# Experts' outputs weighed on the way out of PSUM and added into the tokens' rows in DRAM, with one row per token loaded in the last stage

## The reference

```python
w_topk = w_topk / (jnp.sum(w_topk, axis=-1, keepdims=True) + 1e-06)
...
valid = ranks < capacity
slot = flat_sel * capacity + ranks
...
h = jax.nn.gelu(jnp.einsum('ecd,edf->ecf', padded_x, w1), approximate=False)
out_padded = jnp.einsum('ecf,efd->ecd', h, w2).reshape(N_EXPERTS * capacity, D)
gather_idx = jnp.where(valid, slot, 0)
out_rep = jnp.where(valid[:, None], out_padded[gather_idx], 0.0)
out_w = out_rep * w_topk.reshape(-1)[:, None]
return out_w.reshape(T, TOP_K, D).sum(axis=1).reshape(B, S, D)
...
src = _rmsnorm(src, norm1_w)
src = src + _moe(src, gate_w, w1, w2)
return _rmsnorm(src, norm2_w)
```

## Time and profile before

| | |
|---|---|
| median of 3 runs | 3386.67 us (3379.31 to 3386.76) |
| the profiled execution | 3384.39 us |
| its span, first to last instruction | 3382.7 us |
| experts block | 2759.8 to 3305.1 us |
| combine block | 3305.1 to 3382.7 us |
| PE busy, share of the span | 93% |
| DVE, ACT, POOL busy | 62%, 49%, 33% |
| DMA mean | 110 GB/s; 242 MB read from HBM, 130 MB written |

### The profile page before, as it was taken

One profiled execution on the slowest core, in us unless ns is written; L12 is line 12 of the kernel. 1 busy time (PEld: TensorE's weight loads), 2 busy tenths in 40 slices (PEclk: granted clock), 3 DMA queues, 4 the chain that ended last, 5 costly groups with the idle time before them and its releaser, 6 DMA issues. The chain is left out here.

```text
span 3382.7 us, 58016 instructions
## 1 busy us (share of the span) xinstructions
PE 3135.4 (93%) x18353; PEld 1927.6 (57%) x18353; DVE 2082.6 (62%) x5622; ACT 1663.4 (49%) x3743; POOL 1118.9 (33%) x1508
## 2 busy tenths in 40 slices
PE   7899999999989976999999999999998859999997
PEld 3667767677665653344444444444443348888882
DVE  7777777777772233677777777777777632222226
ACT  3565565655641113666666666666665611111116
POOL 2132232322342123334444444444443322222224
PEclk9999999999999988999999999999999979999998
DMA  8110110101125841112222222222222137777758
GB/s 288 5 73 36 57 51 36 72 36 66 42 88 200 303 169 29 54 54 72 74 73 73 74 73 73 68 73 72 71 73 72 51 99 238 230 235 238 225 169 298
DMA packets 266210, 370.48 MB, mean 110 GB/s; under 512 B 41615, under 2 KB 201579, under 8 KB 263904
## 3 DMA queue, kind: packets, MB, share of 16 engines
q1 hardware_dynamic: 250592, 329.82, 30.2%
q0 software_dynamic: 14832, 34.57, 2.8%
q10 hardware_dynamic: 544, 3.15, 0.2%
HBM read 242.38 MB, written 130.39 MB: 110 GB/s over the span
## 5 line engine op out<-in xcount | busy, mean ns | idle before, releaser
L2425 ACT ACTIVATE pT<-psum 128x512 f32<-128x512 f32 x1024 | 599.1, 599 | 363.2 <-PE psum L3176 348.0
L2709 DVE TENSOR_REDUCE negmax<-psum 128x2 f32<-128x1024 f32 x512 | 624.7, 1220 | 213.8 <-PE psum L3146 198.8
L3176 PE MATMUL psum<-q_stack,k_stack 99*128 99x512 bf16 x1024 | 378.8, 383 | 19.0 <-ACT pT L2425 12.0
L3146 PE MATMUL psum<-k_stack,q_stack 96*128 96x512 bf16 x1024 | 308.1, 382 | 53.7 <-DVE negmax L2709 36.4
L944 ACT ACTIVATE probs<-probs,negmax 128x256 f32<-128x256 f32 x512 | 252.8, 495 | 138.6 <-DVE negmax L1036 135.0
L3492 ACT ACTIVATE actT_x<-psum 128x512 f32<-128x512 f32 x142 | 84.8, 597 | 445.0 <-PE psum L3558 445.0
L3522 DVE COPY ye<-psum 128x512 f32<-128x512 f32 x71 | 49.1, 691 | 400.0 <-PE psum L3570 400.0
L3188 PE MATMUL psum<-pT,v_tile 128*32 128x512 f32 x2048 | 274.3, 608 | 1.0 <-ACT pT L2425 1.0
L3480 POOL DMA_INDIRECT chosen_out<-ye,place x142 | 140.0, 986 | 401.1 <-DVE ye L3522 241.1
L3558 PE MATMUL psum<-xT_x,w_x 128*128 128x256 f32 x1136 | 259.3, 382 | 0.0
L3570 PE MATMUL psum<-w_x,actT_x 128*128 128x256 f32 x1136 | 256.6, 379 | 0.0
(11 more groups left out here) (391 smaller groups left out, 5865.4 us busy)
## 6 DMA issues: line engine op xcount, KB each, us to landing
w_x<-in_L_ffn_w_dram SPq DMA_DIRECT2D x142, 512.0 KB
w_e<-in_L_ffn_w_dram SPq DMA_DIRECT2D x46, 1024.0 KB, 7.2
q_stacks<-q_part SPq DMA_DIRECT2D x192, 128.0 KB
q_stack<-q_stacks SPq DMA_DIRECT2D x64, 384.0 KB, 3.5
padded<-w_e SPq DMA_DIRECT2D x32, 645.0 KB, 5.6
xe<-padded SPq DMA_DIRECT2D x71, 258.0 KB
gate_rows<-mods SPq DMA_DIRECT2D x66, 256.0 KB, 3.3
chosen_out<-w_e SPq DMA_DIRECT2D x16, 1024.0 KB, 7.5
```

What stands on the lines that cost most here:

```text
L2425: act.activation(pT[:, 4 * (s % 2) + r, :], bank(m, 2 + n % 2), ACT.Exp, scale=float(DHQ) ** -0.5)\
L2709: dve.tensor_reduce(negmax[:, p // 2, h:h + 2], m.psum[:, at:at + 2, :], AX.X, ALU.max, negate=True)\
L3146: mm = pe.matmul(bank(m, at + j), q_stack[0:K_SCORE, h, t * P:(t + 1) * P], k_stack[0:K_SCORE, g, :], start=True, stop=True)
L3176: pe.matmul(bank(m, 2 + n % 2), k_stack[:, g, kc * P:(kc + 1) * P], q_stack[:, REP * g + r, :], start=True, stop=True).then_inc(sT_done, 1)
```

## The change

A row of `padded_dram` becomes two numbers longer (260 instead of 258) and carries the token's two weights, and its token number counts tokens and not pairs. In the experts block `place_rows` becomes five small DVE operations, which also work out each row's weight (`weight`), and `copy_out` multiplies by it in two operations of 256 columns. The scatter goes to `src_dram` and adds there (`compute_op=ALU.add`). As two experts may have the same token, the first scatter of tile i waits until both of tile i-1 have landed; the second waits for the first half of the up product of tile i+2, no longer for both. SP waits for `weight` before it loads the rows of tile i+3. The loads of `src_all` leave the experts block.

In the combine block SP issues 16 loads of 512 KB of `src_dram`, all at the start. PE copies each batch to PSUM (no products with expert rows), ACT squares three of the four parts from SBUF, and DVE squares the fourth (`last_square`) and then does the root's steps and the scaling as before. `chosen_out`, its zero stores, the buffer `zeros` and its memset on POOL, and `gather_wt` are gone; in `place` a copy of the weights into `src` takes the place of `valid`, and the product for `gather_wt` is left out.

```diff
@@ routing and rows
-ROW = D + 2
+ROW = D + 4
...
-                sp.dma_start(chosen_out[bass.ds(b * (T * TOPK // B), T * TOPK // B), :]
-                             .rearrange("(p r) d -> p (r d)", p=P), zeros).then_inc(zero_filled, 16)
...
-            pool.memset(zeros, 0.0).then_inc(zeros_ready, 1)
...
-                step(dve.tensor_scalar(valid[:, :, :], rank_k[:, :, :], float(CAP), None, ALU.is_lt))
...
+                step(dve.tensor_copy(src[:, par, :, D + 2:D + 4], wk[:, :, :]))
...
-                step(dve.tensor_tensor(m.gather_wt[:, at], wk[:, :, :].rearrange("p t k -> p (t k)"),
-                                       valid[:, :, :].rearrange("p t k -> p (t k)"), ALU.mult))
@@ experts_block, sync
-                    sp.wait_ge(place_ready, i + 1)
+                    sp.wait_ge(weight_ready, 3 * i + 3)
...
-                if i % 4 == 2 and i // 4 < B:
-                    b = i // 4
-                    sp.dma_start(m.src_all[:, b, :, :], src_dram[b * S:(b + 1) * S, :]
-                                 .rearrange("(t p) d -> p t d", p=P)).then_inc(src_in, 16)
@@ experts_block, gpsimd
                 for t in range(RT):
+                    if t == 0 and i:
+                        pool.wait_ge(sent[(i - 1) % WB], 16 * RT * ((i - 1) // WB + 1))
...
                     if t == 1 and i + 2 < NTILEX:
-                        pool.wait_ge(up_done, 2 * (i + 2) + 2)
-                    pool.indirect_dma_start(chosen_out,
+                        pool.wait_ge(up_done, 2 * (i + 2) + 1)
+                    pool.indirect_dma_start(src_dram,
                                             bass.IndirectOffsetOnAxis(ap=place[:, i % WB, t:t + 1], axis=0),
-                                            ye[:, i % WB, t, :], None, bounds_check=T * TOPK - 1, oob_is_err=False)\
+                                            ye[:, i % WB, t, :], None, bounds_check=T - 1, oob_is_err=False,
+                                            compute_op=ALU.add)\
@@ experts_block, vector
-                dve.tensor_tensor(place[:, u, :], second[:, u, :], xe[:, u, :, D], ALU.add).then_inc(place_ready, 1)
+                dve.tensor_copy(place[:, u, :], xe[:, u, :, D]).then_inc(place_ready, 1)
...
+                dve.tensor_tensor(change[:, :], xe[:, u, :, D + 3], xe[:, u, :, D + 2], ALU.subtract)\
+                    .then_inc(weight_ready, 1)
+                dve.wait_ge(weight_ready, 3 * i + 2)
+                dve.tensor_tensor(change[:, :], change[:, :], second[:, :], ALU.mult).then_inc(change_ready, 1)
+                dve.wait_ge(change_ready, i + 1)
+                dve.tensor_tensor(weight[:, u, :], change[:, :], xe[:, u, :, D + 2], ALU.add).then_inc(weight_ready, 1)
...
-                dve.tensor_copy(ye[:, i % WB, :, :].rearrange("p t d -> p (t d)"), bank(m, 4 + i % 2))\
-                    .then_inc(ye_ready, 1)
+                dve.wait_ge(weight_ready, 3 * i + 3)
+                for t in range(RT):
+                    ins = dve.tensor_scalar(ye[:, i % WB, t, :], bank(m, 4 + i % 2)[:, t * D:(t + 1) * D],
+                                            weight[:, i % WB, t:t + 1], None, ALU.mult)
+                ins.then_inc(ye_ready, 1)
@@ combine_block
-                sp.dma_start(got[:, b % GB, :, :, :].rearrange("p t k d -> p t (k d)"),
-                             chosen_out[b * S * TOPK:(b + 1) * S * TOPK, :]
-                             .rearrange("(t p k) d -> p t (k d)", p=P, k=TOPK)).then_inc(got_in[b % GB], 16)
+                sp.dma_start(m.src_all[:, b, :, :], src_dram[b * S:(b + 1) * S, :].rearrange("(t p) d -> p t d", p=P))\
+                    .then_inc(src_in[b], 16)
...
-                    act.activation(got[:, b % GB, t, 0, :], got[:, b % GB, t, 0, :], ACT.Copy,
-                                   scale=m.gather_wt[:, j:j + 1]).then_inc(first_ready, 1)
...
-                    dve.scalar_tensor_tensor(out=y(b, t), in0=got[:, b % GB, t, 1, :], scalar=m.gather_wt[:, j:j + 1],
-                                             in1=y(b, t), op0=ALU.mult, op1=ALU.add).then_inc(y_ready, 1)
...
+                dve.tensor_tensor_reduce(last[:, :], y(b, NT - 1), m.src_all[:, b, NT - 1, :], scale=1.0 / D, scalar=0.0,
+                                         op0=ALU.mult, op1=ALU.add, accum_out=mean_sq[:, b % 2, NT - 1:NT])\
+                    .then_inc(ms_dve, 1)
```

More of the change, by code:

```diff
@@ L3405, in experts_block @@
         own_f = sb("own_f", [P, RT])
-        second = sb("second", [P, WB, RT])
+        second = sb("second", [P, RT])
+        change = sb("change", [P, RT])
+        weight = sb("weight", [P, WB, RT])
         place = sb("place", [P, WB, RT], U32)
@@ L3638, in store @@
                     .then_inc(stored, 16)
-            for b in range(GB):
+            for b in range(B):
                 load(b)
             for b in range(B):
-                if b + GB < B:
-                    sp.wait_ge(y_ready, (b + 1) * NT)
-                    load(b + GB)
-                if b >= 2:
-                    store(b - 2)
-            store(B - 2)
-            store(B - 1)
+                store(b)
             sp.wait_ge(stored, 16 * B)
@@ L3694, in seed @@
                     act.wait_ge(z_ready, (b - 1) * NT)
[L3695 to L3699 removed]
+                act.wait_ge(src_in[b], 16)
+                for t in range(NT - 1):
+                    act.activation(square[:, t, :], m.src_all[:, b, t, :], ACT.Square, scale=1.0 / 16.0,
+                                   accum_out=mean_sq[:, u, t:t + 1]).then_inc(ms_act, 1)
+                act.wait_ge(ms_act, (b + 1) * (NT - 1))
+                act.wait_ge(ms_dve, b + 1)
                 act.activation(log_ms[:, u, :], mean_sq[:, u, :], ACT.Ln, bias=eps[:, 0:1]).then_inc(log_ready, 1)
```

88 lines of the change are left out of this document (35 added, 53 removed).

## The result

The changed kernel takes 3366.48 us, median of 7 runs (3364.71 to 3373.18), against 3386.76 for the kernel before (3379.31 to 3389.57): a ratio of 0.9946, 95% interval 0.9937 to 0.9955. A second measurement on another chip gave 0.9938 (0.9924 to 0.9951). The profiled execution took 3366.48 us, its span 3364.4.

What follows compares the result with a forecast made beforehand. It took PE to bound the experts block and everything to be tight at once in the combine. From 3384.4 us, -18 (combine), +1.5 (between the blocks) and +7 (experts) gave 3375, in a range of 3362 to 3402.

Steps and rivals of the forecast that it cites:

- What bounds it now: Kernel before: PE bounds the experts block, 98.8 of 100 us busy; in the combine everything is tight at once.
- Combine, -18: Combine block: one DVE operation replaces four, batch 3.72 to 2.55 us, block 77.6 to 59.3; bounds 16.5 to 19.5 less.
- Between the blocks, +1.5: Hand-off from experts to combine: tile 70's scatters wait for tile 69's to land, +1.5 us, bounds 0 and +4.
- Experts block, +7: Experts block: later loads of `xe` cost PE 11 us, less 4 that come back, +7 us; called the softest term.
- item 1: Experts block: SP waits for `weight`, so `xe` is loaded some 0.5 us later and its room falls from 5.0 to 4.5.
- item 2: Experts block: the adding scatter also reads its target, from nothing to 0.56 us more a tile; 0.3 taken ahead of `xe`.
- 20 tiles that pay 0.55: Experts block: PE loses 0.55 us in each of 20 tiles by waiting for `xe`, 11 us.
- item 4: Experts block: the 16 loads of 512 KB leave, each 1.3 us of DMA time just ahead of a load of `xe`.
- Chain of scatters, 0: Experts block: the scatters' chain fits into 7.35 us, cost 0; as a slower rival setting the pace, 3401 us, chance 0.09.
- Two reads: Experts block: the skill's rule that an adding DMA runs at half rate takes POOL's queue from 7.6 to 15%.
- The low clock rival: Combine block: PE at 1.2 GHz sets a batch of 3.75 us, only 4 us less, so 3389 us; chance 0.12.
- Zero stores, `place`, longer rows, 0: Rest of the kernel: dropped zero stores, one DVE operation less in `place` and rows 8 bytes longer change nothing, 0.

Runs made afterwards that it cites:

- a_ms3: The changed kernel with `mean_sq` three batches deep in place of two; ratio 0.9928 to the kernel before, combine 56.3 us.
- a_plain: The changed kernel with scatters that overwrite instead of adding (the addition is left out of the result); ratio 0.9949 to the kernel before.
- after_again: The changed kernel unaltered, run once more as a base; 3352.74 us against 3375.22 for the kernel before, ratio 0.9938.
- a_loads: The changed kernel with sixteen additional 512 KB loads into `src_all` in the experts block, where the kernel before had them; ratio 0.9960 to the kernel before.
- a_nope: The changed kernel with `mean_sq` three deep and no PE in the combine, DVE reading SBUF; ratio 0.9999 to the kernel before, combine 74.9 us.
- after: The changed kernel itself, as first measured and traced; 3366.48 us, ratio 0.9946 to the kernel before.
- a_warm: The changed kernel with `mean_sq` three deep and eight unused small matmuls at the head of PE's combine; ratio 0.9934 to the kernel before, combine 54.3 us.
- a_first_warm: `a_first` with twelve unused small matmuls ahead of PE's first copy; ratio 0.9935 to the kernel before, combine 53.25 us.
- a_first: The changed kernel with `mean_sq` three deep, DVE reading batch 0 from SBUF and scaling it before squaring batch 1; ratio 0.9929 to the kernel before.

## Why the prediction was right, and where it was wrong

- **What bounds it now**: right. PE in the experts block, DVE in the combine.
- **Combine, -18**: measured -17.3, inside the bounds. Two terms were off and nearly cancel. The beginning was counted as 12.4 us and is 9.8: I let DVE start behind both first batches on PE at the low clock, 7.5 us, and only the first was copied at the low clock (its square at 3311.88, 3.6 us behind PE's start; the second's at 3313.59, 1.7 later). The pitch was mis-sized: 2.55, at most 2.65, against 2.83. What I had left out is the wait of DVE for its own scalings, and a_ms3 shows that it was this wait: 2.49 without it. The pair with its accumulator costs 0.36 and not 0.50 (3322.07 to 3322.43); it was the ring of two buffers that cost.
- **Between the blocks, +1.5**: measured +4.2, just over the bound of 4. The step is "landed at about 3298.8, tile 70's last scatter is issued 1.3 later". Without adding, the hand-off grew by 1.0 (a_plain). "Some more for the adding" was meant for the landing; what came were four issues of 1.55 in place of 0.97, 2.3 us, and a wait of tile 69 for the landings of tile 68, 1.0, which I had not counted and which goes back to one issue of 4.07 us.
- **Experts block, +7**: wrong in sign, -4.3. Room fell from 5.0 to 4.5 us as item 1 says, and the adding took 13.1% more of the DMA engines' time, 1.7 times what item 2 allows at most. Together they cost PE one wait of 0.4 us. The step that failed is "20 tiles that pay 0.55": item 4 had named the loads and counted their 4 us, but the tiles that pay were counted as if the loads still stood there. Without them `xe` lands in 3.0 us in the median (after_again), 1.5 less than its room.
- **Chain of scatters, 0**: right in the execution that was measured, and by luck in part. The test, that the chain fits "if the second lands within 6.0 us", leaves out the time from a landing to the next issue and took an issue of 0.97. Measured: 1.85 us from the first issue to the second, and 5.5 from there to the next tile's first (median; the landings take 4.8), 7.35 in all against a tile of 7.344. So there is no room; 53 of 71 first scatters went late, and the buffers of `ye` covered it. With the loads put back the profile names a landing as what POOL waits for 13 times, 59.6 us in all (a_loads), and still PE did not wait for POOL. In the profiled execution of a_nope it did, and the block lost 22 us.
- **Two reads**: the rule gave 15% for POOL's queue, the trace 20.7%, and the block's share is 0.84 and not "about the same" as 0.70. PE did not pay for it in `after`; the scatters' chain did.
- **The low clock rival** did not occur: 1.00 in the middle of the combine. It was at work at the beginning only, where a_warm against a_ms3 and a_first_warm against a_first price it at 1 to 2 us.
- **Zero stores, `place`, longer rows, 0**: what lies ahead of the experts block differs by 0.9 us between the two profiled executions, which can't be told from nothing.

The forecast of 3375 was 8.5 us too high. The three stretches came out +0.7, +2.7 and -11.3 us from their forecasts, 7.9 less together. Nearly all of it is the experts block, which was called the softest term, and which a look at where the ten waits lie would have settled.

## What to carry to other kernels

If an engine waits for a transfer in a few tiles only, look at what else was issued ahead of it in just those tiles before counting the rest as being on the edge; when that thing leaves, the edge leaves too. A stage of a few engines that is busy "8 of 10" everywhere may have a ring of buffers that is one too short, as this one had: read the first small idle time on the engine with the longest list. And an add that moves into a scatter is paid for sure where the scatters must have landed, at the block's end. In the middle of it, work out the whole chain from one tile's first scatter to the next one's, issues and landing and the start of the next: if that is as long as a tile, only buffers hide it, and single executions can lose what the change won.

## What the runs showed of the hardware

- An adding scatter of 128 rows of 1 KB holds POOL 1.55 us and not 0.97, has three times the packets, and takes 2.7 times the DMA time; median landing 4.8 us against 4.0 for an overwriting one at the same place (a_plain).
- DVE and POOL reading only SBUF: a scaling of 0.48 us took 1.98 beside POOL's addition.
- Near it lies an observation that no run here tested: a scatter's issue on POOL that began 2.5 to 3.6 us into DVE's 16 products from SBUF ended 0.85 us (overwriting) or 1.43 us (adding) behind them, in all twelve traces that have one; it took 2.7 to 4.1 us.
- Waiting for its own last scaling, DVE's `last_square` began 0.23 us behind its modelled end; with nothing to wait for, 0.09 ahead of it (a_ms3).
- PE had stood still through the hand-off and was granted 0.53 beside the copy of batch 0; with small matmuls ahead of it, it was granted 0.81 (a_warm), and 1.00 beside that of batch 1 (a_first_warm; 0.50 in a_first).
